# A mixture-of-experts down product in three fp32r passes, its weight parts made in stage one and kept in DRAM

## The reference, cut to what matters

```python
def _L0_ffn_ref(x, gate_w, w1, w2):          # E = 8 experts, H = 512, C = 128
    scores = jnp.einsum('BTC,CE->BTE', x, gate_w)
    probs_et = jnp.transpose(jax.nn.softmax(scores, axis=-1), (0, 2, 1))
    top_p, top_idx = jax.lax.top_k(probs_et, cap)             # cap = 8 of 32 tokens
    xin = jnp.take_along_axis(x[:, None], top_idx[..., None], axis=2)
    h = jax.nn.gelu(jnp.einsum('BElC,ECH->BElH', xin, w1), approximate=False)   # "up"
    y = jnp.einsum('BElH,EHC->BElC', h, w2)                   # "down"
    y = y * top_p[..., None]
    return jnp.zeros((B, T, C), x.dtype).at[b_idx, top_idx].add(y)

x = x + _L0_ffn_ref(_L0_cond_ref(x, cond, ...), gate_w, w1, w2)
```

## Time and profile before

| | us |
|---|---|
| median of 3 runs (550.57 to 550.95) | 550.9 |
| the profiled execution, its time | 550.28 |
| the profiled execution, its span | 549.0 |
| PE busy in the span | 535.7 |
| DVE / ACT / POOL busy | 430.2 / 380.4 / 197.6 |

### The profile page before, as it was taken

How to read it: one execution, slowest core, us unless ns; L and a number is a source line. 1 busy time by engine, 2 the same in 40 slices (tenths; PEclk the granted TensorE clock), 3 DMA queues, 4 the chain that set the end, 5 groups by cost and what they waited for, 6 DMA issues and landing times.

```text
span 549.0 us, 10031 instructions
## 1 busy us (share of the span) xinstructions
PE 535.7 (98%) x3309; PEld 464.1 (85%) x3309; DVE 430.2 (78%) x1042; ACT 380.4 (69%) x857; POOL 197.6 (36%) x186
## 2 busy tenths in 40 slices
PE   8999999999999999999999989999999999999997
PEld 7877888887877899999999877789999999987785
DVE  4987655676868888668756259989999999999866
ACT  5567767768766755344553256988988888888965
POOL 4688788888788203939000000010000000000100
DMA  8634305521090302030000000111111111111211
GB/s 290 192 153 159 153 4 229 193 111 44 1 338 11 135 4 80 0 117 21 1 1 0 1 1 1 27 32 21 20 19 22 20 31 35 36 36 41 49 50 38
DMA packets 30226, 37.35 MB, mean 68 GB/s; under 512 B 20096, under 2 KB 23648, under 8 KB 29280
## 3 DMA queue, kind: packets, MB, share of 16 engines
q1 hardware_dynamic: 30176, 36.72, 20.8%
HBM read 30.24 MB, written 2.28 MB: 59 GB/s over the span
## 4 chain that ended last, share of the span: by engine, by line
PE 80%; DVE 13%; ACT 3%; issue 2%; POOL 2%; DVEq 0%; ACTq 0%
PE bank L325 10%; PE bank L1264 10%; PE bank L326 10%; PE bank L327 10%; PE bank L1689 4%; PE bank L1775 4%; PE bank L1679 4%; PE bank L1716 3%; PE bank L1717 3%; PE bank L1332 2%; PE bank L1214 1%; POOL hidden_low L387 1%; PE bank L1764 1%; PE bank L1802 1%; PE bank L1788 1%
## 5 line engine op out<-in xcount | busy, mean ns | idle before, releaser
L387 POOL TENSOR_TENSOR hidden_low<-hidden,hidden_high 128x512 fp32r<-128x512 f32 x72 | 94.5, 1320 | 21.5 <-ACT hidden_high L372 19.3
L2070 POOL CAST h_high<-h 128x256 fp32r<-128x256 f32 x15 | 6.4, 426 | 197.5 <-ACT h L1881 191.1
L468 ACT ACTIVATE bank<-bank 128x512 f32<-128x512 f32 x56 | 32.6, 583 | 30.4 <-PE bank L327 30.1
L472 DVE TENSOR_TENSOR hidden<-bank,big 128x512 f32<-128x512 f32 x56 | 38.5, 687 | 14.3 <-ACT bank L468 13.3
L372 ACT CAST hidden_high<-hidden 128x512 fp32r<-128x512 f32 x70 | 43.1, 615 | 4.4 <-DVE hidden L472 3.1
L325 PE MATMUL bank<-xin_high,sw_high 128*128 128x256 f32 x128 | 43.9, 343 | 0.0
L1716 PE MATMUL bank<-taps_high,q1T 128*128 128x512 f32 x94 | 42.8, 456 | 1.0 <-ACT q1T L1844 0.6
L1717 PE MATMUL bank<-taps_low,q1T 128*128 128x512 f32 x94 | 37.1, 395 | 0.0
L1817 ACT ACTIVATE gates_t<-bank,lstm_b_half 128x128 f32<-128x128 f32 x96 | 28.2, 364 | 12.1 <-PE bank L1689 8.8
L1398 DVE COPY yT<-bank 128x256 f32<-128x256 f32 x32 | 13.5, 423 | 28.9 <-PE bank L1264 28.9
L1679 PE MATMUL bank<-x,lstm_wx 128*128 128x128 f32 x256 | 34.4, 277 | 1.7 <-ACT gates_t L1817 0.9
(11 more groups left out here) (274 smaller groups left out, 1734.8 us busy)
## 6 DMA issues: line engine op xcount, KB each, us to landing
big<-gates_scratch SPq DMA_DIRECT2D x7, 2048.0 KB, 7.6
w<-in_f_w SPq DMA_DIRECT2D x16, 256.0 KB, 5.9
onehot<-topi_scratch SPq DMA_DIRECT2D x8, 512.0 KB, 4.0
outT<-x SPq DMA_DIRECT2D x15, 128.0 KB, 2.1
xT<-in_xT SPq DMA_DIRECT2D x3, 512.0 KB, 6.9
hidden<-in_ffn_w SPq DMA_DIRECT2D x3, 256.0 KB, 5.3
hidden<-in_conv_w SPq DMA_DIRECT2D x3, 256.0 KB, 4.4
xT<-in_xT SPq DMA_DIRECT2D x2, 256.0 KB, 4.0
```

What stands on the lines that cost most here:

```text
L387: pool.tensor_tensor(hidden_hl[u % 3][1][:, :], hidden[u % 3][:, :], hidden_hl[u % 3][0][:, :].bitcast(F32), ALU.subtract).then_inc(s_lo, 1)
L472: dve.tensor_tensor(hidden[u % 3][:, :].rearrange("p (i k) -> p i k", k=P), r_bank[j % 2][:, :].rearrange("p (i k) -> p i k", k=P), gate_r ...
```

## The change

The down product becomes `product` too: three fp32r matmuls for each fp32 one, with `w2_high`, `w2_low` and a split hidden value. ScalarE now does the gelu in place in PSUM (`expert_gelu`) and a second instruction, `expert_high`, which rounds it to `hb_high`; VectorE does `expert_low` (PSUM minus `hb_high`); there are three buffers of each. The parts of `w1` and `w2` are made once, on VectorE in stage one, at the steps of `PARTS_AT` (12 c + u, that is chunks 2, 3, 4 and 6, with the last in chunk 7). The parts of `w2` stay in place of `w1` and `w2`. Those of `w1` go through two buffer pairs to a DRAM scratch, and are read back for each expert and group into three buffer pairs. The high parts are made by `tensor_tensor` with a zero operand. The orders of SP, VectorE and ScalarE in the groups are rewritten to hold this.

```diff
+            w1_dram = nc.dram_tensor("w1_parts_scratch", [E, 2, P, H0], F32, kind="Internal").ap()
...
+                    if n * c + u in PARTS_AT:
+                        w1_high_part(PARTS_AT.index(n * c + u))
+                    if n * c + u - 1 in PARTS_AT:
+                        w1_low_part(PARTS_AT.index(n * c + u - 1))
+                    if n * c + u - 3 in PARTS_AT:
+                        w2_high_part(PARTS_AT.index(n * c + u - 3))
+                    if n * c + u - 4 in PARTS_AT:
+                        w2_low_part(PARTS_AT.index(n * c + u - 4))
...
+            PARTS_AT = (25, 31, 37, 43, 49, 55, 74, 80)
...
+            def w1_high_part(e):
...
+                dve.tensor_tensor(w1_parts[e % 2][0][:, :], w1[:, e, :], zero[:, 0:1].to_broadcast([P, H0]), ALU.add
+                                  ).then_inc(s_w1hi, 1)
...
+            def load_parts(k):
...
+                if k >= 3:
+                    sp.wait_ge(s_h, 2 * (k - 2))
+                for part_no, dst in enumerate(w1_hl[k % 3]):
+                    sp.dma_start(dst[:, :].bitcast(F32), w1_dram[k % E, part_no]).then_inc(s_w1ld[k % 3], 16)
...
-            def expert_split(k):
...
-                dve.tensor_copy(high[:, :], w1[:, e, :]).then_inc(s_es, 1)
-                dve.wait_ge(s_es, 2 * k + 1)
-                dve.tensor_tensor(low[:, :], w1[:, e, :], high[:, :].bitcast(F32), ALU.subtract).then_inc(s_es, 1)
...
             def expert_down(w):
...
-                pe.wait_ge(s_hg, w + 1)
+                pe.wait_ge(s_hbl, w + 1)
...
-                    mm = pe.matmul(y_bank[e % 2][:, 0:SLOT_GE], w2[:, e, ht, :], hb[w % 4][:, i * SLOT_GE:(i + 1) * SLOT_GE],
-                                   start=(ht == 0), stop=(ht == HT - 1))
+                    h_parts = [hl[w % 3][:, i * SLOT_GE:(i + 1) * SLOT_GE] for hl in (hb_high, hb_low)]
+                    mm = product(y_bank[e % 2][:, 0:SLOT_GE], (w2_high[:, e, :], w2_low[:, e, :]),
+                                 slice(ht * P, (ht + 1) * P), h_parts, ht == 0, ht == HT - 1)
                 mm.then_inc(s_y2, 1)
+
+            def expert_gelu(w):
+                act.wait_ge(s_h, w + 1)
+                act.activation(h_bank[w % 4][:, :], h_bank[w % 4][:, :], ACT.Gelu).then_inc(s_hg, 1)
+
+            def expert_high(w):
+                act.wait_ge(s_hg, w + 1)
...
+                if w >= 3:
+                    act.wait_ge(s_y2, w - 2)
+                act.copy(hb_high[w % 3][:, :], h_bank[w % 4][:, :]).then_inc(s_hbh, 1)
+
+            def expert_low(w):
+                dve.wait_ge(s_hbh, w + 1)
...
+                dve.tensor_tensor(hb_low[w % 3][:, :], h_bank[w % 4][:, :], hb_high[w % 3][:, :].bitcast(F32), ALU.subtract
+                                  ).then_inc(s_hbl, 1)
...
-                    if g == 0 and u == 1:
+                    expert_gelu(w)
+                    expert_high(w)
+                    if g == 0 and u == 4:
                         choice_exp(1)
```

More of the change, by code:

```diff
@@ L150, in build_program @@
             iota_tok = sb0("iota_tok", [P, P])
-            part = sb0("part", [P, 1])
+            part, zero = sb0("part", [P, 1]), sb0("zero", [P, 1])
             seq_off = sb0("seq_off", [P, 2, SEQ_TILE, CAP])
@@ new lines, in build_program, with w2_raw @@
+            PARTS_AT = (25, 31, 37, 43, 49, 55, 74, 80)
+            STORE_PARTS = {2: (0, 1), 3: (2, 3), 4: (4, 5), 5: (), 6: (), 7: ()}
+            s_w1hi, s_w1lo, s_w2hi, s_w2lo = (sem(n) for n in ("s_w1hi", "s_w1lo", "s_w2hi", "s_w2lo"))
+            s_w1st = [sem(f"s_w1st{k}") for k in range(2)]
+            w1_parts = (w1_third, (hb_third, ctok_low0))
+            s_w1ld = [sem(f"s_w1ld{k}") for k in range(3)]
+            def w2_raw(e):
+                return w2[:, e, :, :].rearrange("p f c -> p (f c)")
@@ new lines, in w2_high_part, with w2_low_part, store_parts @@
+            def w2_high_part(e):
+                dve.wait_ge(s_w1lo, e + 1)
+                dve.tensor_tensor(w2_high[:, e, :], w2_raw(e), zero[:, 0:1].to_broadcast([P, H0]), ALU.add
+                                  ).then_inc(s_w2hi, 1)
+            def w2_low_part(e):
+                dve.wait_ge(s_w2hi, e + 1)
+                dve.tensor_tensor(w2_low[:, e, :], w2_raw(e), w2_high[:, e, :].bitcast(F32), ALU.subtract
+                                  ).then_inc(s_w2lo, 1)
+            def store_parts(e):
+                sp.wait_ge(s_w1lo, e + 1)
+                for k in range(2):
+                    sp.dma_start(w1_dram[e, k], w1_parts[e % 2][k][:, :].bitcast(F32)).then_inc(s_w1st[e % 2], 16)
@@ L1034, in first_chunks_sp @@
             def first_chunks_sp():
-                load_expert(0)
-                load_expert(1)
+                for e in range(4):
+                    load_expert(e)
                 sp.wait_ge(s_gtc, 1)
@@ L1153, in build_program @@
             onehot, ctok_hl = [], []
-            w1_hl = (sw1_hl, sw3_hl)
+            w1_hl = (sw1_hl, sw3_hl, w1_third)
+            hb_high = [nc.alloc_sbuf_tensor_at(f"hb{k}_high", [P, CHUNK], F32R, offset=at_th + 4 * CHUNK * k) for k in range(2)] + [hb_third]
+            hb_low = [nc.alloc_sbuf_tensor_at(f"hb{k}_low", [P, CHUNK], F32R, offset=at_pb + 4 * CHUNK * k) for k in range(2)] + [ctok_low0]
             def chosen(g, par):
@@ L1482, in group_dve @@
                         residual(g - 1, 0)
+                    output_copy(g, e)
+                    if w + 3 < GROUPS * U2 and not (g and e == 1):
+                        expert_low(w + 3)
+                    if g and e == 1:
                         residual(g - 1, 1)
-                    if g < GROUPS - 1:
-                        if e in (1, 3):
-                            tokens_low(g + 1, e // 2)
-                        if e in (2, 4):
-                            gather_onehot(g + 1, e // 2 - 1)
@@ L1489, in group_dve @@
-                    tables_at = 2 if g == GROUPS - 1 else 4
+                    if g < GROUPS - 1 and e in (1, 3):
+                        gather_onehot(g + 1, e // 2)
+                        tokens_low(g + 1, e // 2)
                     if tables_at <= e < tables_at + 4:
                         scatter_tables(g, range(4 * (e - tables_at), 4 * (e - tables_at + 1)))
-                    if k + 3 < GROUPS * E and not (g and e == 1):
-                        expert_split(k + 3)
-                    output_copy(g, e)
+                    if g == 0 and e == 2:
+                        choice_probs(1)
@@ L1505, in group_dve @@
+                    if g == 0 and e == 5:
+                        for k in range(1, 4):
+                            weight_sum(k)
                     if g == 0 and e == 6:
@@ L1521, in build_program @@
                     prepare_weights()
-                if g == GROUPS - 2:
-                    for k in range(3):
-                        load_tap(k)
             slots_turn_late()
```

149 lines of the change are left out of this document (94 added, 55 removed).

## The result

The changed kernel takes 570.22 us (median of 4 runs, 567.2 to 571.71) against 550.74 of the kernel before (4 runs, 550.29 to 550.95). The ratio is 1.035, with a 95% interval of 1.032 to 1.038: slower, as forecast, but by 19.5 us and not by 6, and outside the range. The profiled execution is the fastest of the four, 567.2, with a span of 565.9 at a granted clock of 1.00; the other three ran at 0.993 to 0.994.

A forecast was written before the change was run, and what follows sets the result against it. TensorE was taken as full in stage one and the expert stage. Sum: 550.28 - 8.9 + 8.1 + 1.8 + 0.5 + 5 = 556.8 us profiled, 557.4 as median, stated as 557; range 550 to 564, the forecast's own 553.5 to 562.

The forecast's parts named there:

- the gain: Expert stage, TensorE: a step takes 1.44 us rather than 1.57, a gain of 0.14, times 64 steps: -8.9 us.
- group 0, in order: Expert stage, group 0: seven TensorE waits counted from strict ScalarE and VectorE lists, together +8.1 us, bounds 3 and 11.
- every turn of group: Between groups: slots_out on ScalarE delays the next group's first gelu; three turns of 0.6, +1.8 us.
- beside GpSimd in group 1: Group 1: VectorE's one-hot and token work beside GpSimd's preparation costs +0.5 us, bounds 0 and 2.
- elsewhere in groups 1 to 3 I find room: Groups 1 to 3, apart from turns and VectorE's work beside GpSimd: no further cost counted.
- stage one: Stage one: 32 new two-operand VectorE operations and GpSimd's hidden_low exclude each other; +5 us, bounds 0 and 14.
- GpSimd has 3.3 us free in a chunk, and eight delays of about 0.55 make 4.4: over by 1.1: Stage one, first estimate of the port's cost: 1.1 us over in each of four chunks, 4.4 us.
- My second estimate: Stage one: from two chunks already holding such operations, 0.22 us each, times 32: 7.0 us.
- The rule of the Trainium skill: SBUF: VectorE and GpSimd share a port pair as an exclusive lock, taken also by VectorE operations with two SBUF inputs.
- the tap loads' new place on SP: SP queue: tap loads ahead of weight loads; GpSimd's preparation begins about 6 us later, and nothing waits for it.
- from profiled execution to median: Whole kernel: the median of the runs lies 0.6 us above the profiled execution.
- The rival of late weight parts: Expert stage: weight parts landing over 6.5 us after their buffer frees make TensorE wait, 562 to 570 us; chance 0.15.

The follow-up runs named there:

- e4: Kernel before with only the down product in three fp32r passes, low parts left out and other tiles read as weight parts: 541.77 us, ratio 0.983.
- e6: e3 with group 0's choice transposes at step 11, weight sums at experts 3 and 5, and means ahead of the scatter tables: 563.46 us.
- e3: Changed kernel with the copy of group 1's second slot columns moved ahead of its expert's four scatter tables on VectorE: 568.21 us.
- e5: e3 with the one-hot table and token subtraction ahead of the output copy and second residual sum on VectorE in groups 1 and 2: 561.76 us.
- e1: Changed kernel with 28 of stage one's 32 new VectorE operations replaced by one-operand sums; the down product reads other parts: 560.4 us.
- e8: Changed kernel with the four edits of e3, e5, e6 and e7 together: 554.81 us, ratio to the kernel before 1.0075.
- e9: e8 with the rounding of w1 on ScalarE: 552.12 us, ratio to the kernel before 1.0033.
- e11: e10 with the first one-hot table and token subtraction ahead of the second expert's output copy in group 0 too: 550.22 us, ratio 0.9991 to the kernel before.
- e2: Changed kernel with 28 of stage one's 32 new VectorE operations on 4 columns, not 512; the down product reads other parts: 563.87 us.
- e7: Changed kernel with the 16 operations making w2's parts moved from VectorE in stage one to GpSimd in group 0: 567.2 us.
- e10: e9 with the subtraction of w1 on GpSimd, behind hidden_low of the same unit: 553.66 us, ratio to the kernel before 1.0051.

## Why the prediction was right in sign and wrong in size

Term by term, for the profiled execution (550.28 before, 556.8 forecast, 567.2 measured):

| step of the prediction | forecast | measured | shown by |
|---|---|---|---|
| the gain | -8.9 | -9.8 | e4, without its own two waits |
| group 0, in order | +8.1 | +7.8 | waits after; e6 |
| every turn of group | +1.8 | +1.6 | waits after |
| beside GpSimd in group 1 | +0.5 (0 to 2) | +2.8 | e3 |
| "elsewhere in groups 1 to 3 I find room" | 0 | +2.8 | e5 |
| stage one | +5 (0 to 14) | +8.9 | e1 |
| from profiled execution to median | +0.6 | +3.0 | granted clock of the runs |

The measured terms without the last make 564.4; 2.8 us of the 567.2 remain. They lie in the expert stage, beside the printed waits: against e4 without its two waits, group 0 is 9.1 us longer and not 7.8, and groups 1 and 2 together 8.0 and not 6.7 (e5 gave back 4.2 for 2.8 of waits there). So a sum of printed waits is too low by a sixth here.

The term of the gain has a slip, too: 1.57 less 1.44 is 0.13 and not 0.14, 8.3 us in all. The down product's own difference, 0.86 less 0.72, gives the 0.14.

**The strict count of group 0 held.** Seven waits were named with place and size, and seven were there (1.31 for 1.65, 0.60 for 0.5, 1.66 for 1.1, 1.40 for 1.5, 0.22 for 0.3, 1.44 for 1.55, 1.13 for 1.5). The sum is closer than its terms (0.56 too little at `choice_transpose`, 0.34 and 0.37 too much at down(5) and the turn), which is luck. Reading each in-order list against TensorE's pays.

**Stage one: right mechanism, term mis-sized.** The failed step is "GpSimd has 3.3 us free in a chunk, and eight delays of about 0.55 make 4.4: over by 1.1". It counts the delays of one engine, and gives 5 us where e1 gives 8.6 for 28 of the 32 operations (8.9 in all). The trace after shows the delays on both engines: the 32 operations lasted 35.9 us instead of 32 times 0.68, and `hidden_low` 7.0 more. And the hidden value passes through both in turn: VectorE multiplies, ScalarE rounds, GpSimd subtracts. ScalarE's rounding waited for VectorE 14.7 us in this stage, before 4.3. My second estimate, 0.22 an operation from chunks that already held such operations, was nearer; e1 gives 0.31. The rule of the Trainium skill ("SBUF — State Buffer", SBUF: two separate sides) that I had set against the change holds in e1: the four operations left with two SBUF operands took 1.18 to 1.72 us there. `tensor_reduce` never contends on this chip, as the Trainium skill says ("SBUF — State Buffer", Who interferes with whom), and the trace of e1 agrees: it took 0.67 to 0.69 in all 28 cases.

**Group 1: the bound of 2 us was too low.** I had looked at the one-hot and token work that meets GpSimd, and not at the scatter tables, which are slowed from 1.11 to 3.0 us for four (3.2 in e3), nor at who stands behind them in VectorE's list: the rewritten order put the slot columns there. And of the tap loads' new place on SP the prediction says that nothing waits for it. SP and GpSimd, before and after:

```profile
242.29 9.55 SPq L211 DMA_DIRECT2D hidden<-in_conv_w  x3
...
246.81 0.72 POOL L261 TENSOR_SCALAR hidden<-hidden,wmean 128x512 f32<-128x512 f32 x1 [9.10 <-DMA hidden<-in_conv_w]
```

```profile
252.23 0.90 SPq L218 DMA_DIRECT2D hidden<-in_conv_w  x2
...
256.34 0.70 POOL L268 TENSOR_SCALAR hidden<-hidden,wmean 128x512 f32<-128x512 f32 x1 [4.97 <-DMA hidden<-in_conv_w]
```

Counted from `slots_turn(0, 0)` (213.98 and 229.83), the loads were issued after 28.3 us before and 22.4 now, and GpSimd began the taps after 32.8 and 26.5. Before, VectorE had by then done the copy of the slot columns (245.86). So the loads' new place put taps and tables together, and not group 0's delay, which moves both. This is read from the two traces; no run moves the loads alone.

**"Elsewhere I find room" failed** at one place: I checked ScalarE's busy share, not what its second token rounding waits for. That is VectorE's token subtraction, behind two residual sums.

**The median.** I added 0.6 us as in the kernel before. The profiled run had a clock of 1.00 and the other three 0.993 to 0.994; that this is the 3 us is argued from these figures, and no trace shows where in those three the clock was low.

The rival of late weight parts did not decide anything: a wait of 0.2 to 0.9 us for a part at one expert shows in e1, e5, e8, e9 and e11, and none in the changed kernel's own trace.

## What to carry to other kernels

Before work is put into an engine's free time, ask which port it uses, and add the delay of both engines that meet there: here the same number of VectorE instructions cost 8.9 us or 0.3. A list that is counted strictly for one stretch has to be counted so for all stretches: the waits in groups 1 and 2, at two places for which I had 0.5 us, add up to 5.6, and two edits of order gave back 6.7. And a change whose gain is in one engine's slots needs its helper instructions placed, not only fitted: the same kernel with the weight parts on GpSimd and ScalarE and a few instructions reordered is 20 us faster than the changed one, and then only even with where it began.

## What the runs showed of the hardware

Two engines at SBUF. Beside GpSimd's work, VectorE's 128x512 operations with two SBUF operands took 1.0 to 1.26 us on average, with one 0.68, a `tensor_reduce` 0.67 to 0.69; four scatter tables took 2.6 to 3.2 and not 1.11, a one-hot table 1.44 and not 0.75.

The granted clock. It fell in some executions, a few us at a time: in the profiled ones of e2, e6, e7 and e10 in the expert stage, in that of e3 only behind it (0.53 at 364 to 366 us, behind waits of TensorE of 0.85 and 1.04). In all five the fall came right behind waits of TensorE. Mean clocks were 1.00, 0.994, 0.993 and 0.994 in the changed kernel, 0.984 to 0.997 in e2, 0.987 to 0.994 in e7. At the lower level a matmul of 256 columns starts every 0.21 us, as here in e2, and a few lines later every 0.12:

```profile
207.54 0.42 PE L339 MATMUL bank<-hb_high,xin_low 128*128 128x256 f32 x1
207.75 0.41 PE L337 MATMUL bank<-hb_high,xin_high 128*128 128x256 f32 x1
...
209.31 0.28 PE L339 MATMUL bank<-xin_high,w_third_low 128*128 128x256 f32 x1
209.43 0.28 PE L337 MATMUL bank<-xin_high,w_third_high 128*128 128x256 f32 x1
```

The fall is not certain. The changed kernel's profiled run has waits up to 2.76 us and a clock of 1.00, and e1, with the same waits but for the first, had 1.00 in all four runs; e10, whose longest waits in this stage are 1.24 and 1.34, had 0.990 in three of six. Even the kernel before shows 0.996 in six of its 21 runs beside e9 to e11, with a spread of 2.8 us (549.72 to 552.5). So a wait of TensorE may cost some us beyond its length in part of the executions: the changed kernel spreads over 4.5 us in four runs where the one before spreads over 0.7. That the waits cause the falls is argued, and what decides in which execution the clock falls stays open.
